# Attention scores on the loaded keys and queries in plain fp32, in a stack of LoRA layers and paged attention

## The reference

```python
q = rope(rmsnorm(x @ Wq.T)); k = rope(rmsnorm(x @ Wk.T)); v = x @ Wv.T
kc = k_cache[block_table].reshape(bsz, L, HK, D)      # L = 16 pages * 32 = 512
vc = v_cache[block_table].reshape(bsz, L, HK, D)
k_all = concatenate([kc, k]);  v_all = concatenate([vc, v])      # 544 keys
scores = einsum('bqhd,bkhd->bhqk', q, k_all) * SCALE
scores = where(valid, scores, -1e30)
probs = softmax(scores)
o = einsum('bhqk,bkhd->bqhd', probs, v_all)
return einsum('bse,de->bsd', o, Wo)
```

## Time and profile before

| | |
|---|---|
| median of three runs | 2888.45 us |
| span of the profiled execution | 2886.1 us |
| instructions | 58057 |
| TensorE busy, of the span | 2721.6 us (94%) |
| VectorE, ScalarE, POOL busy | 2042.3, 1441.0, 1352.4 us |
| attention, from its first score matmul to its last output | 1005.8 to 2510.6 us |
| data moved | 507.06 MB, 176 GB/s on average |

### The profile page before, as it was taken

The page is one execution under the profiler, slowest core; times in us unless marked ns, Lnnn a source line. Parts: engine busy times, 40 slices in busy tenths (PEclk is TensorE's granted clock), DMA queues, the critical chain, the costliest instruction groups (busy, mean ns, idle before and its releaser), DMA issues. The chain is left out here.

```text
span 2886.1 us, 58057 instructions
## 1 busy us (share of the span) xinstructions
PE 2721.6 (94%) x16646; PEld 2298.8 (80%) x16647; DVE 2042.3 (71%) x3956; ACT 1441.0 (50%) x2637; POOL 1352.4 (47%) x1008
## 2 busy tenths in 40 slices
PE   7699899999999589999999999999999999799999
PEld 5587677777777478888888888888888888778887
DVE  5355339999999678888888888888888888542221
ACT  3222234444444366666666666666666666431111
POOL 1222165665565555566666666555666666200000
PEclk9899899999999799999999999999999999999999
DMA  6422432332332488887778888888877888353332
GB/s 221 128 76 69 159 109 89 92 102 84 89 89 77 146 248 237 243 237 229 231 237 236 237 234 237 240 236 242 237 229 231 237 236 236 110 208 117 137 109 84
DMA packets 364201, 507.06 MB, mean 176 GB/s; under 512 B 56547, under 2 KB 269731, under 8 KB 360292
## 3 DMA queue, kind: packets, MB, share of 16 engines
q1 hardware_dynamic: 336036, 416.54, 49.2%
q0 software_dynamic: 25984, 86.79, 8.7%
q10 hardware_dynamic: 2112, 2.89, 0.3%
HBM read 407.98 MB, written 98.04 MB: 175 GB/s over the span
## 5 line engine op out<-in xcount | busy, mean ns | idle before, releaser
L1303 POOL TENSOR_TENSOR att_k_lo<-att_k_raw,att_k_hi 128x1024 fp32r<-128x1024 f32 x256 | 606.0, 2367 | 502.4 <-ACT att_k_hi L1337 502.3
L1395 DVE TENSOR_SCALAR att_prob<-att_prob,att_inv_total 128x544 f32<-128x544 f32 x512 | 635.8, 1242 | 0.0
L1329 ACT ACTIVATE att_pt<-att_ps_pt 128x512 f32<-128x512 f32 x512 | 305.8, 597 | 497.6 <-PE att_ps_s L1476 497.6
L1488 PE MATMUL att_ps_o<-att_pt,att_v 128*128 128x128 f32 x4096 | 541.2, 275 | 0.0
L1488 PEld LDWEIGHTS att_ps_o<-att_pt,att_v 128*128 128x128 f32 x4096 | 497.9, 192 | 6.4
L884 POOL TENSOR_TENSOR qkv_part_b<-qkv_normed,qkv_cross 128x256 f32<-128x256 f32 x320 | 297.6, 951 | 240.3 <-DVE qkv_normed L1044 240.3
L1322 ACT ACTIVATE att_prob<-att_prob,att_shift 128x544 f32<-128x544 f32 x512 | 378.4, 739 | 0.0
L76 PE MATMUL att_ps_s<-att_k_hi,att_q_hi 128*128 128x272 f32 x1024 | 349.1, 341 | 26.5 <-POOL att_k_lo L1303 26.1
L1383 DVE CUSTOM_DVE_ANT_0 att_prob<-att_ps_s,att_mask 128x544 f32<-128x544 f32 x512 | 360.2, 704 | 2.2 <-PE att_ps_s L78 2.2
L1473 PE MATMUL att_ps_pt<-att_ident,att_prob 128*128 128x128 f32 x2048 | 318.6, 278 | 23.0 <-DVE att_prob L1395 12.4
L76 PE MATMUL qkv_ps_y<-qkv_w_hi,qkv_xt_hi 128*128 128x512 f32 x768 | 320.2, 417 | 0.0
(11 more groups left out here) (174 smaller groups left out, 4893.5 us busy)
## 6 DMA issues: line engine op xcount, KB each, us to landing
att_k_raw<-in_k_pages SPq DMA_DIRECT2D x1024, 128.0 KB, 3.9
att_v<-in_v_pages SPq DMA_DIRECT2D x1024, 128.0 KB, 3.1
q_t<-qkv_out_t SPq DMA_DIRECT2D x128, 256.0 KB, 2.3
att_q_raw<-q_t POOLq DMA_DIRECT2D x64, 512.0 KB, 4.1
o_t<-att_o POOLq DMA_DIRECT2D x64, 512.0 KB, 6.2
out_o<-o_t SPq DMA_DIRECT2D x32, 1024.0 KB, 6.5
qkv_w_stage<-in_w_qkv SPq DMA_DIRECT2D x12, 1024.0 KB, 5.2
l_w_stage<-in_w SPq DMA_DIRECT2D x8, 1024.0 KB, 7.0
```

The lines of the kernel that those rows point to most:

```text
L1303: pool.tensor_tensor(lo, raw, f32(hi), ALU.subtract).then_inc(pool_split, 1)
L1329: act.activation(pt_sb[:, j % 2, :, :], ps_pt[:, j % 2, :, :], ACT.Copy).then_inc(pt_ready, 1)
L1395: dve.tensor_scalar(prob[:, b, :], prob[:, b, :], inv_total[:, b:b + 1], None, ALU.mult)\
L1488: pe.matmul(out, v_sb[:, p, c, h * DH:(h + 1) * DH], pt_sb[:, j % 2, c, :], start=(c == 0), stop=False)
```

## The change

Queries and keys are no longer split. `k_hi`, `k_lo`, `q_hi`, `q_lo`, the pieces and their semaphores `hi_done`, `pool_split`, `dve_split` are gone. TensorE multiplies `q_raw` with `k_raw` directly, in two plain fp32 matmuls a unit, one over 9 pages (288 keys) and one over 8 (256 keys); each page contributes 32 neighbouring keys of the head, pages lie 256 elements apart. The two halves now end and begin at one bank border of `ps_s`, so that DVE reads 544 neighbouring elements. The raw buffers are now read by the score matmuls themselves, and so every load into them waits for `s_done`.

```diff
-                    for c in PIECE_TURN:
-                        if c in CACHED:
-                            if later(s, 2):
-                                sp.wait_ge(pool_split, ON_POOL * (s - 2) + c + 1)
-                            first, n = pages_of(c)
-                            for at in range(first, first + n):
-                                sp.dma_start(k_raw[:, p, at, :], k_pages[bass.ds(pages[at], 1)])\
-                                  .then_inc(k_loaded[p][c], 16)
+                    if later(s, 2):
+                        sp.wait_ge(s_done, HK * (s - 1))
+                    for at, page in enumerate(pages):
+                        sp.dma_start(k_raw[:, p, at, :], k_pages[bass.ds(page, 1)]).then_inc(k_loaded[p], 16)
...
                 def load_q(s, p):
                     if later(s, 2):
-                        pool.wait_ge(pool_split, ON_POOL * (s - 2) + PIECE_Q + 1)
+                        pool.wait_ge(s_done, HK * (s - 1))
...
                 def load_own_k(s, p):
                     if later(s, 2):
-                        pool.wait_ge(dve_split, s - 1)
+                        pool.wait_ge(s_done, HK * (s - 1))
...
                     for p in range(2):
                         s = 2 * i + p
-                        for c in range(ON_POOL):
-                            raw, hi, lo = piece(c, p)
-                            pool.wait_ge(hi_done, PIECES * s + PIECE_TURN[c])
-                            pool.tensor_tensor(lo, raw, f32(hi), ALU.subtract).then_inc(pool_split, 1)
+                        load_own_v(s, p)
                         if not last:
                             load_q(s + 2, p)
                             load_own_k(s + 2, p)
-                        load_own_v(s, p)
                         if later(s, 2):
                             store(s - 2, p)
...
                     if h == 0:
-                        pe.wait_ge(pool_split, ON_POOL * (2 * i + p + 1))
-                        pe.wait_ge(dve_split, (PIECES - ON_POOL) * (2 * i + p + 1))
+                        pe.wait_ge(k_loaded[p], 16 * NPP * (i + 1))
+                        pe.wait_ge(q_loaded[p], 16 * (i + 1))
+                        pe.wait_ge(own_k_loaded[p], 16 * (i + 1))
...
-                    for half in range(2):
-                        keys = slice(half * HALF, (half + 1) * HALF)
-                        mm = three_pass(pe, ps_s[:, j % 2, half, 0:HALF], q_hi[:, p, h, :], q_lo[:, p, h, :],
-                                        k_hi[:, p, h, keys], k_lo[:, p, h, keys], True, True)
+                    q = q_raw[:, p, h * P:(h + 1) * P]
+                    for half, (first, n) in enumerate(((0, FIRST_PAGES), (FIRST_PAGES, NPP + 1 - FIRST_PAGES))):
+                        at = 0 if half else SPLIT
+                        mm = pe.matmul(ps_s[:, j % 2, half, at:at + n * PSIZE].rearrange("p (n k) -> p n k", n=n), q,
+                                       k_raw[:, p, first:first + n, h * PSIZE:(h + 1) * PSIZE], start=True, stop=True)
```

More of the change, by code:

```diff
@@ L1145 @@
 OG = 4
[L1148 to L1163, removed]
+FIRST_PAGES = 9
+SPLIT = D - FIRST_PAGES * PSIZE
 def attention(nc, pool_sems, k_pages, v_pages, table, lens, key_at, q_t, k_own, v_own, o_t):
@@ L1195, in attention @@
         q_loaded, own_k_loaded, own_v_loaded, o_stored = pool_sems
-        k_loaded = [m.sems(f"k_loaded{p}_", PIECE_Q) + [q_loaded[p]] + m.sems(f"k_loaded{p}__", 1) + [own_k_loaded[p]]
-                    for p in range(2)]
+        k_loaded = m.sems("k_loaded", 2)
         v_loaded = m.sems("v_loaded", 2)
-        hi_done = m.sem("hi_done")
-        pool_split, dve_split = m.sem("pool_split"), m.sem("dve_split")
         s_done = m.sem("s_done")
@@ L1207, in attention @@
         o_ready = m.sem("o_ready")
-        def piece(c, p):
-            if c == PIECE_Q:
-                return q_raw[:, p, :], *(b[:, p, :, :].rearrange("p h q -> p (h q)") for b in (q_hi, q_lo))
-            first, n = pages_of(c)
-            return (k_raw[:, p, first:first + n, :].rearrange("p n (h k) -> p n h k", h=HK),
-                    *(b[:, p, :, first * PSIZE:(first + n) * PSIZE].rearrange("p h (n k) -> p n h k", n=n)
-                      for b in (k_hi, k_lo)))
         with nc.Block() as block:
@@ L1329, in copy_pt @@
                     act.activation(pt_sb[:, j % 2, :, :], ps_pt[:, j % 2, :, :], ACT.Copy).then_inc(pt_ready, 1)
[L1331 to L1342, removed]
                 exponential(0, 0)
@@ L1351, in pair @@
                             exponential(u + 2, (j + 2) % UNITS)
[L1352 to L1355, removed]
                 in_pairs(act, NSEQ // 2, pair)
@@ L1383, in mask_and_max @@
                     dve.tensor_tensor_reduce(
-                        out=prob[:, b, :].rearrange("p (a n) -> p a n", a=2), in0=ps_s[:, j % 2, :, 0:HALF],
-                        in1=mask[:, j // HK, :].rearrange("p (a n) -> p a n", a=2), scale=-SM_SCALE, scalar=3e38, op0=ALU.add, op1=ALU.min,
+                        out=prob[:, b, :], in0=ps_s[:, j % 2, :, :].rearrange("p a n -> p (a n)")[:, SPLIT:SPLIT + NALL],
+                        in1=mask[:, j // HK, :], scale=-SM_SCALE, scalar=3e38, op0=ALU.add, op1=ALU.min,
                         accum_out=shift[:, b:b + 1]).then_inc(masked, 1)
@@ L1411, in copy_o @@
                        .then_inc(o_ready, 1)
[L1413 to L1419, removed]
                 for j in range(2):
@@ L1437, in pair @@
                             normalise(u + 1, j + 1)
-                        if not (last and j >= HK):
-                            for c in DVE_PIECES_AT[j % HK]:
-                                split_lo(2 * i + j // HK + 1, 1 - j // HK, c)
                         if j % OG == 1:
```

7 lines of the change are left out of this document (2 added, 5 removed).

## The result

The changed kernel takes 3553.55 us (median of 4 runs, 3550.91 to 3556.97) against 2889.25 us for the kernel before in the same series: a ratio of 1.2298, 95% interval 1.2281 to 1.2316. The forecast was 3415 us in a range from 3285 to 3560, slower. The direction, the place and the mechanism held; the time lies 139 us above the forecast, 6 us under the top of the range.

A forecast was written before the change was run, and what follows sets the result against it. TensorE was taken as the bound before the change, waits for late values after it. Attention ends at 1022 + 62 x 32.0 + 24 + 7.5 = 3037.5 instead of 2510.6, +527 us: 3415 us, range 3285 to 3560.

The forecast's parts named there:

- The decisive term: Load waits on SP's in-order queue: values stand behind keys held until t0; TensorE stands still 7.8 us a sequence.
- t0: Moment in attention when the last scores of sequence s are done and its key buffer is free; first at 1022 us.
- Scores: Two plain fp32 matmuls a unit on TensorE: two clocks a column, 1.05 us, 0.19 us dearer than before.
- U: One TensorE turn in attention: scores 1.05, transposes 0.54, outputs 1.40, in all 2.99 us.
- Start: Start of attention: transposes near 1007 us instead of 1018.65, first t0 at 1022.
- The late values: Values of s+1 whole 20.3 us after t0: waking 0.1, issues 9.04 and 7.83, page numbers 0.7, last landing 2.6.
- The store: Store behind POOL's query loads: issued 1.5 us after t0, `pto_ready` at 10.0, hidden by the values' wait; uncovered, P = 29.0.
- P: Period of one sequence in attention: 20.3 + 11.4 = 31.7 us, with 0.3 for the clock 32.0, in place of 23.3.
- The clock: TensorE's low clock behind idle gaps: covered behind the first, up to 2.3 us behind the second; 0.3 us a sequence entered.
- Rival B: Low clock behind every gap in attention, 2.3 us instead of 0.3 a sequence: 124 us more, 3539 us; chance 0.07.
- A: Key and value transfers catch up, values within 12.5 us of t0: 3229 us; chance 0.08; store early too, 2913, 0.01.
- C: Plain score records paced by weight load, 0.60 us a unit: 2686 us if values and store are early; chance 0.02.

The follow-up runs named there:

- experiment 3: Changed kernel with both orders turned round, values ahead of keys on SP and store ahead of queries on POOL: 2901.83 us, ratio 1.0043.
- experiment 5: Kernel before, splits and fp32r scores kept, only the cached keys of s+2 wait for the last scores of s: 3633.5 us, ratio 1.2577.
- Experiment 4: Changed kernel with values issued by POOL at the same time as SP's keys, and the store ahead of them: 3556.9 us, ratio 1.2312.
- experiment 1: Changed kernel with SP issuing the values of s+1 ahead of the keys of s+2: 3456.39 us, ratio 1.1955.
- experiment 2: Changed kernel with POOL issuing the store of s-2 ahead of the query and own-key loads: 3753.77 us, ratio 1.2982.
- experiment 6: Kernel of experiment 1 plus twelve useless matmuls in the turn that waits for the store: 3318.74 us, ratio 1.1491.

## Why the prediction was right, and where it was off

**The decisive term held.** Keys of s+2 wait for t0, values of s+1 stand behind them, TensorE stands still, and the store stands behind the queries: all four are in the queues above, and experiments 3 and 5 show them from both sides (turned round, 652 us go; one wait alone, 745 us come).

**Scores.** Forecast 1.05 us a unit and U = 2.99; measured 1.02 and 2.97. Two clocks a column, read from one row of the first layer, was right. From the values to the next t0 the forecast and the measurement are both 11.4 us.

**Start.** Transposes forecast near 1007, measured 1006.72; first t0 forecast 1022, measured 1021.6.

**The late values: the term that was undersized.** Forecast 20.3 us after t0, measured 22.8 in the sequence shown. Waking and issues were near: 0.33 us instead of 0.1, 8.88 and 7.84 us, and 1.36 us of page numbers in this sequence, where the mean of 0.7 was entered (the next one has almost none and still gets its values 22.1 us after t0). The term that was off is "2.6 for the last to land": it was 4.4. I took the median landing of all pages, but the last page of a sequence is later than the median: already in the kernel before, it landed 3.3 us after the end of the issues on average. And that trace has keys and values in separate stretches; here both, the queries and the store are asked for back to back, and the DMA engines' share is 1.07 from 1926 to 1934. Experiment 4 shows that this backlog, and not SP's pace of issue alone, sets when the values are whole. Counted in bytes the term comes out: 5.5 MB at the measured 245 GB/s are 22.5 us.

**The store: right in kind, too short.** `pto_ready` forecast 10.0 us after t0, measured 11.7: 2.25 us to the store's issue instead of 1.5, and 7.0 from there to DVE's copy instead of 6.2. Its cover is thinner than the forecast's 2.7 us: with the slow turn, TensorE wants the values 21.6 us after t0 and gets them at 22.8. In 55 of the 62 sequences the values' landing decides, in seven the slow turns behind the store. So the store did cost nothing as long as the values were that late, as forecast, but the sum without that cover was wrong: P = 29.0 forecast, 33.0 in experiment 1.

**The clock.** The forecast entered 0.3 us a sequence, and held that a low clock behind the first gap is covered. It is covered (experiment 2), up to the wait for values, which is about 1 us long in most sequences. Rival B's 2.3 us behind every gap was about right as a price: 2.2 and 3.0 us in experiments 6 and 2; it was wrong for the place.

**The sum.** P was 34.2 us (the queries' issues are 34.22 us apart on average over 61 sequences) instead of 32.0; 62 x 2.22 = 138 us, all but 1 of the 139 us between forecast and result. The late landing alone does not explain it: with the values in time (experiment 1) the time is 3456 us, still 41 above the forecast, and the period 33.0, because the store's wait and the low clock behind it make a chain longer than 32.0 by themselves. Of the 2.2 us about 1.0 is that chain's and 1.2 the values'. All the terms that were off were too low, and that the result is still inside the range, 6 us under its top, is in part luck: the top was set by rival B's price for the clock, not by a later landing or a longer store.

**Rivals.** A (transfers catch up) did not occur; experiment 4 shows the engines at 242 GB/s for this mix, with a share of 1.01, even with two queues feeding them; keys and values within 12.5 us would have taken 335. The room of 292 GB/s, scaled up from a share of 0.79, was not there either: the share grew faster than the rate. That the Trainium skill's 408.7 GB/s for larger transfers (page "DMA: Bandwidth & Descriptors", section "iDMA fabric"), quoted in the prediction, can be had here, no run shows. C (cheap plain records) fell with the scores' 1.02 us.

## What to carry to other kernels

When a consumer starts to read a raw buffer directly, its release moves from the end of the copy to the end of the consumer; look then at what stands *behind* every load into it in the same in-order queue, and put what waits for nothing ahead of it. Two orders of issue were worth 652 of 3554 us here, and either one alone 98 and -200. And do not judge a wait by its total: remove it and see what comes next, and on which side of the remaining wait the slow clock falls.

## What the runs showed of the hardware that was not expected

Removing a gap of TensorE of some 6.6 us in each sequence made the kernel 200 us slower (experiment 2), and 5.8 us of useless matmuls in each sequence made another 138 us faster (experiment 6): behind gaps of 6 to 10 us TensorE worked for a while at a lower granted clock, with plain fp32 scores taking 1.94 us instead of 1.02.

Landing times depend on what else is asked for: a 128 KB value page took 3.1 us in the median before, 4.1 in the changed kernel and 6.8 when keys and values were issued side by side.
